# A decoder layer on one core: front transform as a GpSimd butterfly and smaller products, two steps reordered, two inverses moved to VectorE

## The reference

```
x = x + attention(layernorm(x))          # 8 heads, rope, causal, mixed with a "geometric" softmax
x = x + wkv(layernorm(x), ctx)           # "context": a decaying scan over the 128 tokens, per channel
x = x + ffn(layernorm(x))

wkv:   y_t = (e1*aa + e2*v_t) / (e1*bb + e2)      # numerator over denominator, per token
ffn:   h_bitlinear(a, w) = act_quant(fwht(a)) @ weight_quant(w).T
       gate, up = h_bitlinear(a, w_gate), h_bitlinear(a, w_up)
       out = h_bitlinear(silu(gate) * up, w_down)
fwht:  Walsh-Hadamard transform of the last axis (256 before gate/up, 1024 before down), normalised
act_quant: per token, scale = 127 / max|a|, round to integers, divide by scale
```

## Time and profile before

| | us |
|---|---|
| median of 3 runs | 423.54 |
| lowest, highest | 423.49, 425.12 |
| the profiled execution | 422.08 |
| its span in the profile | 420.3 |
| TensorE busy | 358.9 |
| VectorE busy | 341.8 |
| ScalarE busy | 267.3 |
| GpSimd busy | 139.3 |

### The profile page before, as it was taken

One profiled execution on the slowest core, in us unless ns is written; L12 is line 12 of the kernel. 1 busy time (PEld: TensorE's weight loads), 2 busy tenths in 40 slices (PEclk: granted clock), 3 DMA queues, 4 the chain that ended last, 5 costly groups with the idle time before them and its releaser, 6 DMA issues.

```text
span 420.3 us, 7763 instructions
## 1 busy us (share of the span) xinstructions
PE 358.9 (85%) x2369; PEld 254.5 (61%) x2386; DVE 341.8 (81%) x936; ACT 267.3 (64%) x532; POOL 139.3 (33%) x160
## 2 busy tenths in 40 slices
PE   1958899999998999989989686879989999998994
PEld 0735565556554566546656484757767777776773
DVE  4594999999999999999988768968798979888531
ACT  1252787877877777777785655676575858574442
POOL 1212144244552344433641424323233334333200
PEclk9976999999999999999999996979999999999897
DMA  7970003000000000000000000000000000000001
GB/s 218 289 252 2 0 2 115 12 14 16 12 15 0 15 13 14 14 2 14 12 15 13 2 2 1 0 0 2 27 1 25 2 27 12 15 12 13 14 25 40
DMA packets 13712, 13.44 MB, mean 32 GB/s; under 512 B 2007, under 2 KB 12887, under 8 KB 13543
## 3 DMA queue, kind: packets, MB, share of 16 engines
q1 hardware_dynamic: 13671, 12.94, 10.2%
HBM read 10.84 MB, written 2.10 MB: 31 GB/s over the span
## 4 chain that ended last, share of the span: by engine, by line
PE 36%; DVE 34%; issue 17%; ACT 7%; DMA 1%; SPq 1%; POOL 1%; DVEq 1%; ACTq 0%; POOLq 0%
PE wide L712 8%; PE bank L940 6%; PE wide L830 4%; PE wide L697 3%; DVE a_g_diag L1274 3%; DVE c_z L1049 2%; DVE a_att L1280 2%; PE wide L721 2%; ACT c_q2T L471 2%; DVE c_hh L1058 2%; DVE c_am L1071 2%; PE bank L727 2%; DVE a_rot_s L1226 2%; PE wide L799 2%; PE wide L822 2%
## 5 line engine op out<-in xcount | busy, mean ns | idle before, releaser
L408 POOL TENSOR_TENSOR c_h_lo<-c_hb,c_h_hi 128x512 fp32r<-128x512 f32 x32 | 41.0, 1282 | 77.5 <-ACT c_h_hi L460 72.2
L712 PE MATMUL wide<-had,c_h_hi 128*128 128x512 f32 x128 | 54.8, 428 | 7.3 <-ACT c_q2T L471 7.3
L712 PE MATMUL wide<-had,c_h_lo 128*128 128x512 f32 x128 | 52.0, 406 | 0.0
L697 PE MATMUL wide<-c_q_T,w_tern_all 128*128 128x256 bf16 x256 | 37.5, 290 | 7.6 <-DVE c_hh L1058 6.6
L453 ACT ACTIVATE c_sl<-c_z 128x512 f32<-128x512 f32 x32 | 20.2, 630 | 32.3 <-DVE c_z L1049 32.3
L940 PE MATMUL bank<-w_o,a_att 128*128 128x256 f32 x128 | 31.8, 391 | 6.3 <-DVE a_att L1280 5.8
L384 POOL TENSOR_TENSOR b_ev_in<-b_e_in,b_vT 128x256 f32<-128x256 f32 x16 | 21.7, 1353 | 45.9 <-ACT b_e_in L514 45.9
L697 PEld LDWEIGHTS wide<-c_q_T,w_tern_all 128*128 128x128 bf16 x256 | 24.3, 103 | 18.5 <-DVE c_hh L1058 8.5
L712 PEld LDWEIGHTS wide<-had,c_h_hi 128*128 128x128 f32 x128 | 24.9, 195 | 14.0 <-issue 9.1
L940 PEld LDWEIGHTS bank<-w_o,a_att 128*128 128x128 f32 x128 | 23.1, 189 | 16.1 <-DVE a_att L1280 12.7
L373 POOL TENSOR_TENSOR a_qk<-a_rot_c,a_rot_s 128x320 f32<-128x320 f32 x16 | 15.7, 983 | 49.1 <-DVE a_rot_s L1226 49.1
(11 more groups left out here) (186 smaller groups left out, 1004.0 us busy)
## 6 DMA issues: line engine op xcount, KB each, us to landing
x_res<-in_x SPq DMA_DIRECT2D x4, 512.0 KB, 7.3
b_vT<-in_ctxT SPq DMA_DIRECT2D x16, 128.0 KB, 2.3
out<-c_yo SPq DMA_DIRECT2D x16, 128.0 KB, 1.7
w_raw_all<-in_wg SPq DMA_DIRECT2D x1, 1024.0 KB, 8.2
w_raw_all<-in_wu SPq DMA_DIRECT2D x1, 1024.0 KB, 10.3
w_raw_all<-in_wd SPq DMA_DIRECT2D x1, 1024.0 KB, 12.8
had_f<-in_h SPq DMA_DIRECT2D x1, 1024.0 KB, 4.9
w_o_raw<-in_Wo SPq DMA_DIRECT2D x4, 128.0 KB, 6.4
```

Source lines behind the costliest of these rows:

```text
L408: nc.gpsimd.tensor_tensor(h_lo[p][:, j::FQ, :], hb[j % 2][:, :].rearrange("c (m t) -> c m t", m=2), h_hi[p][:, j::FQ, :].bitcast(F32), ALU ...
L697: mm = nc.tensor.matmul(dst[:, m * TOK:(m + 1) * TOK], w[:, k * FF + blk * P:k * FF + blk * P + P], q_T[p][:, k * TOK:(k + 1) * TOK], star ...
L712: mm = nc.tensor.matmul(wide[:, 1 + i, m * 512:(m + 1) * 512], a[p][:, j + FQ * m, i * P:(i + 1) * P], had512[:, j, :], start=(j == 0 and ...
```

## The change

Per pair, GpSimd forms lo + hi and lo - hi of the normalised channels into a new buffer c_xb (`butterfly`, two instructions of 128x256), `turn_x` turns c_xb instead of c_xn, and `transformed` is four products of 128x128 (a quarter of had256) without accumulation. GpSimd's butterfly of pairs 2 to 7 stands between low(m,0) and low(m,1); that of pair 0 ahead of its attention round 16, that of pair 1 behind attention round 17. In the rounds, turn2(b,1) moves ahead of transformed(f) on TensorE; scale2(b,1) ahead of turned(f), and turned2(b,1) ahead of silu 2, on ScalarE. `finish` is gone; the inverses of context blocks 14 and 15 are reciprocals by VectorE, three context steps ahead of its feed of round 2 and three behind it. The idle products before the fourth up group of pair 0 become 10 instead of 4.

```diff
-def woven(attention, pair, finish=None):
+def woven(attention, pair):
     for r in range(NB + 3):
         attention(r)
-    pair(1)
-    pair(2)
-    if finish:
-        finish()
-    for r in range(3, NP + 3):
+    for r in range(1, NP + 3):
         pair(r)
...
+        c_xb = two("c_xb", [P, 2, C])
...
+                def butterfly(u, p):
+                    need(pool, D["xn"], 2 * (u + 1))
+                    need(pool, D["t"], u - 1)
+                    lo, hi = c_xn[p][:, :, 0:P], c_xn[p][:, :, P:C]
+                    nc.gpsimd.tensor_tensor(c_xb[p][:, :, 0:P], lo, hi, ALU.add).then_inc(D["xb"], 1)
+                    nc.gpsimd.tensor_tensor(c_xb[p][:, :, P:C], lo, hi, ALU.subtract).then_inc(D["xb"], 1)
...
                         normal(*f)
                     if m is not None:
                         low(*m, 0)
+                    if f is not None and f[0] > 1:
+                        butterfly(*f)
                     if m is not None:
                         low(*m, 1)
...
                     if r == NB - 1:
                         normal(0, 0)
+                    if r == NB:
+                        butterfly(0, 0)
                     body(*slots(r, NB, 5))
+                    if r == NB + 1:
+                        butterfly(1, 1)
...
                 def normed(u, p):
                     need(act, D["shift"], u + 1)
-                    need(act, D["t"], u - 1)
+                    need(act, D["xb"], 2 * (u - 1))
...
                         high(*m, 0)
+                    if b is not None:
+                        scale2(*b, 1)
                     if f is not None and f[0] > 1:
                         turned(*f)
-                    if b is not None:
-                        scale2(*b, 1)
                     if m is not None:
                         high(*m, 1)
-                    if m is not None:
-                        silu(*m, 2)
                     if b is not None:
                         turned2(*b, 1)
+                    if m is not None:
+                        silu(*m, 2)
...
-                def finish():
-                    nc.scalar.preload_act_table_set("natural_log_exp_and_others")
-                    for u in (NB - 2, NB - 1):
-                        context_inverse(u, u % 2)
...
                         if u == 0 and j and s_free == "h":
-                            idle_work(scoresT, 4)
+                            idle_work(scoresT, 4 if j < 3 else 10)
...
                 def turn_x(u, p):
-                    need(pe, D["xn"], 2 * (u + 1))
+                    need(pe, D["xb"], 2 * (u + 1))
...
-                            mm = nc.tensor.transpose(c_turn[:, at:at + P], c_xn[p][:, i, k * P:k * P + P], ident[:, :])
+                            mm = nc.tensor.transpose(c_turn[:, at:at + P], c_xb[p][:, i, k * P:k * P + P], ident[:, :])
...
-                            mm = nc.tensor.matmul(hx[u][:, i * C:(i + 1) * C], x3T[p][:, (2 * k + i) * P:(2 * k + i + 1) * P],
-                                                  had256[:, k, :], start=(k == 0), stop=(k == KC - 1))
+                            mm = nc.tensor.matmul(hx[u][:, i * C + k * P:i * C + (k + 1) * P], x3T[p][:, (2 * k + i) * P:(2 * k + i + 1) * P],
+                                                  had256[:, 0, 0:P], start=True, stop=True)
...
                         gate_up(*m, 2)
+                    if b is not None:
+                        turn2(*b, 1)
                     if f is not None and f[0] > 1:
                         transformed(*f)
                     if b is not None:
-                        turn2(*b, 1)
...
                 def denominator(u, p):
...
-                    need(dve, B["ln"], u)
+                    need(dve, B["ln"], min(u, NB - 2))
+                    if u == NB - 1:
+                        need(dve, B["inv"], u)
...
+                def quotient(u, p):
+                    need(dve, B["dnm"], u + 1)
+                    need(dve, B["y"], u - 1)
+                    nc.vector.reciprocal(invb[p][:, :], dnm[p][:, :]).then_inc(B["inv"], 1)
+
                 def pair(r):
                     if r == 2:
                         scans(NB - 1, (NB - 1) % 2)
+                        quotient(NB - 2, NB % 2)
+                        context_now(NB - 2, NB % 2)
+                        denominator(NB - 1, (NB - 1) % 2)
                     feed(*slots(r, NP, 4))
-
-                def finish():
-                    denominator(NB - 1, (NB - 1) % 2)
-                    context_now(NB - 2, NB % 2)
-                    numerator(NB - 1, (NB - 1) % 2)
-                    context_now(NB - 1, (NB - 1) % 2)
+                    if r == 2:
+                        numerator(NB - 1, (NB - 1) % 2)
+                        quotient(NB - 1, (NB - 1) % 2)
+                        context_now(NB - 1, (NB - 1) % 2)
```

More of the change, by code:

```diff
@@ L278, in decoder_layer @@
         down = [bank[0][:, 0:C], bank[1][:, 0:C]]
-        names = ("st6 eps mv mneg shift ve rstd xn t x3T hx am amc rcp qs rs fac qm qb dg ts qT srow g u z sl h bf hi lo had "
+        names = ("st6 eps mv mneg shift ve rstd xn xb t x3T hx am amc rcp qs rs fac qm qb dg ts qT srow g u z sl h bf hi lo had "
                  "am2 r2 rcp2 qs2 os qm2 t2 q2T dn yo").split()
@@ L665, in attention @@
                         turned(1, 1)
-                def finish():
-                    nc.scalar.preload_act_table_set("natural_log_exp_and_others")
-                    for u in (NB - 2, NB - 1):
-                        context_inverse(u, u % 2)
-                woven(attention, lambda r: feed(*slots(r, NP, 4)), finish)
+                woven(attention, lambda r: feed(*slots(r, NP, 4)))
             @block.tensor
```

5 lines of the change are left out of this document (2 added, 3 removed).

## The result

The changed kernel takes 450.57 us (median; 450.26 to 452.79) against 423.58: ratio 1.0649, 95% interval 1.0602 to 1.0696. The direction was as forecast, the size was not: plus 27 us against plus 7.6, far outside the range. Medians and ratios from here on leave out runs over 1.5% above the fastest of the same kernel; two of j_unorder's six are such, its profiled one among them. The profiled execution took 450.38 us with a span of 448.6, 28.3 more than the span before. Those 28.3 us are the sum explained here.

The account below looks back on a forecast made before the run. Bound: the longest loop through nearly full TensorE and VectorE, lengthened by GpSimd's queue. Five rounds +7.0, first pair +4.0, second -0.5, inverses +0.5, tail -3.4: plus 7.6 on 423.54 gives 431.1 us, range 425.5 to 435.5.

Parts of the forecast that it names:

- The place and cause of the waits: TensorE's turn of the front idles some 3.4 us per round, because the butterfly stands behind GpSimd's low part.
- the allowance of 0.3: Added to the butterfly's 1.4 us in each round, because VectorE and GpSimd share a port.
- The reduction at 11.8 us behind the mark: VectorE's scale reduction comes 11.8 us after the round's first gate product, against 9.2 before: 2.6 us later.
- The first pair's price, plus 4.0: Attention round 16: the first butterfly, behind GpSimd's power, ends at 220.65 and delays a turn that ran at 216.73.
- The tail: From round 8 on, turning the second half's block earlier on ScalarE saves 3.4 us (1.8 to 3.6).
- that wait goes, 8.96 remain: From scale reduction to next round's mark, VectorE's 0.95 us wait vanishes, leaving 8.96 of 9.91 and a 20.7 us round.
- the second pair's butterfly at 0.4 lost: After attention round 17: 0.4 us lost at the shared port (0 to 0.7), 0.9 gained by the transform, net minus 0.5.
- I cost it as line 1063, 0.42 us: Context inverses: a 128x256 reciprocal on VectorE takes 0.42 us, six instructions 2.4 us, the whole part plus 0.5.
- as the forecast, and the reciprocals take 2.1 us each: Rival: forecast plus slower reciprocals, or the butterfly held 0.6 us in seven places; 433 to 435 us, chance 0.10.
- The first rival, a hidden butterfly: The butterfly is hidden in the rounds and TensorE's smaller work counts: 409 us, chance 0.12.
- The second rival, a loss in attention that later waits take up: Later waits absorb the attention delay and the port never holds the butterfly: 424.9 us, chance 0.08.
- TensorE's relief: The transform drops from 1.78 to 0.89 us per pair; in the rounds the forecast said this does not pay.

Follow-up runs that it names:

- j_unorder: The changed kernel with TensorE's and ScalarE's order as before (transform ahead of the second half's turn): 452.05 us, ratio 1.0658.
- c_idle: The changed kernel with products of no use on TensorE ahead of its wait for the butterfly: 441.78 us, ratio 1.0398.
- d_first: The changed kernel with GpSimd's butterfly ahead of its first low part, and pair 0's in attention round 15 ahead of the power: 424.40 us, ratio 0.9999.
- m_both: c_idle with VectorE's residual(b, 0) moved ahead of hidden(m, 2): 437.74 us, ratio 1.0301.
- e_inverse: d_first with the two context inverses by ScalarE and the step between rounds 2 and 3 as in the kernel before: 422.39 us, ratio 0.9971.
- i_bfly: The kernel before with only the butterfly (first in GpSimd's round), the 128x128 products and the idle products; order and inverses as before: 423.81 us, ratio 1.0025.
- k_idle10: The kernel before with only the idle products ahead of pair 0's fourth up group raised from 4 to 10: 424.25 us, ratio 0.9989.
- a_recip: The kernel before with only the two context inverses moved to VectorE and the step between rounds 2 and 3 removed: 426.67 us, ratio 1.0053.
- b_order: The kernel before with only the reorder: second half turned ahead of the transform, its scaling and turned copy earlier on ScalarE: 421.28 us, ratio 0.9940.
- h_order_resid: b_order with VectorE's residual(b, 0) moved ahead of hidden(m, 2): 419.96 us, ratio 0.9920.

## Why the prediction was right in sign and wrong in size

**Right.** The place and cause of the waits: 3.98 us at the first pair's turn, 3.3 to 3.6 in rounds 4 to 7 (in rounds 2 and 3 only 1.8 and 1.7), all for a butterfly behind GpSimd's low part or its power. The transform at 0.9 us (0.91 on the chain at full clock, in c_idle), no wait for c_q2T, no table load between rounds 2 and 3. The butterfly's end, 8.58 us behind the mark in round 7 (388.17 to 396.75) where 8.6 was forecast: the allowance of 0.3 was of the right size, though it is spread over both instructions (0.91 and 0.90 against 0.74 and 0.73 in d_first) and not a delay ahead of them. The reduction at 11.8 us behind the mark: 11.99 at full clock. The first pair's price, plus 4.0, at full clock: 3.93.

**Right by luck.** The tail: minus 4.0 against minus 3.4. At the same clock the order gives 1.8 to 2.3, the lower end of the 1.8 to 3.6 that was laid out; the rest is that the execution before had its tail at 0.89 and the one after at 0.95.

**Wrong, and by how much.** Added up, the misses close the gap between plus 7.6 and plus 28.3:

1. *Missing from the sum: what TensorE's clock does after the waits.* The forecast made every step with durations at full clock; rounds 4 to 7 and the attention stretch of before were at 1.00. It put a wait of 3 to 4 us ahead of every turn, and did not ask what the engine would be granted afterwards, though the trace of before has it: rounds 1 to 3 at 0.85 to 0.90, and behind the wait of 3.04 us four records at 1.03 us that take 0.61 at full clock. It cost 7.2 us in rounds 3 to 7 (117.8 less c_idle's 110.5), 2.1 in the attention step (6.1 less 4.0), and 3.3 in the stretch behind it (26.96 less m_both's 23.68): 12.6 us together, three fifths of the miss. The last 3.3 are the least certain, for in kernels without the change the same stretch differs by as much from profile to profile (22.8 to 25.9 us).
   The other 0.9 us of that stretch are there at full clock too. The forecast put the second pair's butterfly at 0.4 lost; what the 0.9 are made of wasn't looked into.
2. *Step "that wait goes, 8.96 remain".* It stayed, at 0.96. VectorE isn't simply behind TensorE in the second half of the round, since TensorE in its turn waits there for VectorE: 0.67 us for the residual, through the shared bank. The forecast took the wait for c_q2T out of TensorE's round and didn't ask what TensorE would meet next. In the trace before, the tie shows not as a wait but as a small margin; VectorE's residual and TensorE's turned-back rows stand at

```profile
354.21 0.48 DVE L1098 SCALAR_TENSOR_TENSOR c_yo<-bank,c_os,x_res 128x256 f32<-128x256 f32 x1
```

and

```profile
354.99 0.39 PE L763 MATMUL bank<-ident_b,c_qb 128*128 128x128 bf16 x4
```

so the residual ends at 354.69 and its reader starts 0.3 us later, and TensorE could get only that much earlier before it had to wait for it. Of the 0.95 a run gives back 0.45 (m_both); what holds the other half is open. In size: 9.77 instead of 8.96, and 11.99 instead of 11.8, or 21.75 for a round instead of 20.7: 1.05 us a round, 5.3 in five.
3. *Step "I cost it as line 1063, 0.42 us".* The reciprocal took 1.73. The estimate from the Trainium skill's page "VectorE: DVE Perf Modes", section "First, the fixed hardware budget", was 2.1 us; that was nearer. My reading of a reciprocal of two elements was a poor test: by the two sizes measured an element costs 6.2 ns, 12 ns for two of them out of 166. Rounds 1 and 2 came out at plus 2.5 instead of nothing: the inverses cost 1.8 to 1.9, the late butterfly in round 2 another 1.8 (41.41 in the change against 39.63 in d_first), and the smaller transforms with an early butterfly give back 1.2 (e_inverse 37.75 against 38.94 before).
4. *The tail* gave 0.6 more than the forecast, by the clock, as said above.

12.6 + 0.9 + 5.3 + 2.5 - 0.6 = 20.7 on top of 7.6 is 28.3, against 28.3. The terms are differences between single profiled executions of several kernels, so that they close so well is in part chance.

The rival that came nearest, "as the forecast, and the reciprocals take 2.1 us each", had the reciprocals right and went no further than 435. The first rival, a hidden butterfly, is d_first: with the queue in the right order rounds 4 to 7 do hide all but 0.64 us, and it still gives 424.4 and not 409. The second rival, a loss in attention that later waits take up, is refuted by the marks: nothing of the first stretch's 6.1 us was given back. TensorE's relief is worth nothing in a round: 19.39 in i_bfly and 19.24 in d_first against 19.10.

What stays open: why the clock held in round 5 and fell in rounds 6 and 7 with waits of the same length (3.3 us); why the same code up to the last rounds of attention gets a different clock in different profiles; what holds the other half of VectorE's wait; and what the order is worth in the changed kernel at full clock (c_idle with the old order wasn't tried).

## What to carry to other kernels

Before giving work to the engine with the most idle time, look at what stands ahead of it in that engine's queue and at what the consumer would do meanwhile: the same two instructions made the kernel 26 us slower behind other GpSimd work than ahead of it (450.57 and 424.40). A wait that is added to TensorE is to be priced at its length plus what the clock does behind it, with the slow level's durations, and if it can't be avoided, products without use in it are worth trying. And before striking out a wait because its engine "is now late", follow the releaser one round back: if the releaser waits for that same engine, both move together and the wait, or half of it, can stay. Last, before a stretch is called faster or slower between two profiles, compare its granted clock: the tail here looked 4.0 us better and was 1.8 to 2.3.

## What the hardware did that was not expected

- The clock. The eight records of the second half's turn stand at 1.04 us in a stretch at 1.00, the 2.4 GHz level, and at 1.92 right behind a wait (398.65), in a stretch of 0.66 on average, that is partly at the 1.2 GHz level. After waits of 3.3 us the granted clock fell in rounds 6 and 7 (0.93) and not in round 5 (343.02 to 364.76, 1.00). Between rounds 5 and 6 that makes 1.7 us (21.74 and 23.41) for the same work and the same wait.
- Products without use ahead of an unavoidable wait made the kernel 8.8 us faster (450.57 to 441.78), while PE's busy time in a round rose from 17.28 to 20.40 us (round 5). Where TensorE wasn't waited for, holding its clock up gave nothing (k_idle10: 0.85 to 0.92 in round 1, 17.81 us in both).
- The same code ran the same stretch of attention at 1.00, 0.93 or 0.87, in 22.8, 24.3 and 25.9 us (a_recip, b_order, h_order_resid), with nothing altered in or ahead of it.
- A reciprocal of 128x256 takes 1.73 us and one of 128x2 0.166: some 6.2 ns for each further element ((1.73 - 0.166) / 254), where a tensor_scalar or product of that many elements takes 0.42 in all.
- A butterfly instruction of 128x256 on GpSimd takes 0.74 and 0.73 us ahead of the low part (d_first) and 0.91 beside VectorE's lines 1069 and 1070, which have two SBUF inputs; line 1070 loses at the same time (0.94 for 0.42). The forecast had one side held and the other not.
